# Attention outputs turned by 32x32 block transposes on VectorE instead of transposes on TensorE, in a one-core decoder layer

## The chip, the core and the metric

The kernel runs on one core of a Trainium2 chip. A core has TensorE (matmuls and its own transposes, PE in the rows, with its weight loads as PEld), VectorE (DVE), ScalarE (ACT), GpSimd (POOL) and SyncE (SP, which issues most transfers). Each engine works through its own queue in order and waits on semaphores that the others raise. The metric is the device time of one execution in microseconds (us); lower is better.

## What is computed

One post-norm decoder layer on 16 sequences of 256 tokens with 256 features and 16 heads of 16 features: causal self attention with normalised and rotated queries and keys, causal cross attention to a second sequence with a key mask, and a feed-forward part of two branches (1024 and 128 wide). Cut to what matters here:

```python
qkv = x @ w_qkv.T                       # split into q, k, v of 16 heads
attn = softmax(q @ k.T * 16 ** -0.5)    # causal, per head
out = einsum('bhqk,bhkd->bhqd', attn, v)
out = out.transpose(0, 2, 1, 3).reshape(B, T, 256)
x1 = layernorm(x + out @ w_proj.T)      # self attention; the cross attention
x2 = layernorm(x1 + cross @ Wo)         # is the same with k, v of the context
x3 = layernorm(x2 + ffn(rmsnorm(x2)))
```

## The kernel before

Everything of one sequence (a "batch" b) stays in SBUF. Each engine's program is one Python function `step(i)`, written out for i = -2 to 19, and the order within it is set by hand. In step i the batches are s = i for self attention, c = i - 1 for cross attention, f = i - 2 for the end of cross attention, l = i - 3 for the feed-forward part, and i + 1 and i + 2 for the next q, k and v.

TensorE's step has four phases of 16 heads each, called here **S1** (scores of self attention for s), **S2** (scores of cross attention for c), **T1** (transposed scores of s, which become probabilities) and **T2** (transposed scores of c). Between the heads `phase()` puts other work: for each position h it first issues what tables like `OUT1_AT`, `QK1_AT` or `HIDDEN_AT` assign to h, in the order in which it was added, and then head h. The scores of all phases go round a ring of three PSUM banks (`wait_ring`): a score tile of S1 or S2 may be written when VectorE has taken the maximum (`mx`, L931) of the tile three before it, one of T1 or T2 when ScalarE has taken its exponential (L763). Every matmul is recorded at L359, whatever calls it; the row's tiles tell them apart: `cmaskb,idb` opens a head of S1 or S2, `stk1q,stk1k` and `stk2q,stk2k` are heads of T1 and T2, `pr,va` the values of a group of four heads, `wo,onT` the output projection.

The path of an attention output, for a = 1 (self) and a = 2 (cross): `values` (L530) leaves four groups of four heads with features on partitions, each head in its own 32 of them (16 features, the sum of its probabilities, 15 zeros); ScalarE copies each group to `oT` (`copy_group`, L717). When all four are there, `out_tokens` (L554) turns them to tokens on partitions with eight TensorE transposes (L585), `normalise_heads` on VectorE (L964) takes the reciprocal of the sums and multiplies (L968, L975), `out_dims` (L589) turns the result back with four transposes (L386), ScalarE copies that to `onT` (`copy_out`, L711), and `out_proj` (L595) multiplies with the output weights. For self attention this runs within T2 of the same step: values of the last group at position 3, tokens at 4, back at 8, projection at 10 (`OUT1_AT`); the second half of the q/k projection `qk1` stands at 9. For cross attention it runs in S1 of the next step, at 3, 5, 10 and 12 (`OUT2_AT`).

ScalarE's T2 loop takes, per head, the squares of the q/k projection ahead of heads 5 and 10 (`SQ_AT`, L862) and then the exponential. VectorE's order at the end of a step is: remainder of the cross keys (`take_rest`, L907), `normalise_heads(1, s)`, the split of that remainder, the third layer norm, the two sums of squares (L1037), the residual and statistics of the first layer norm, one Newton step of the inverse root, the first layer norm's output (L1012, which needs a root from GpSimd, L1239), two more Newton steps; then step i + 1 begins with the maxima of S1, with the scaling of q and k at heads 1 and 2, `normalise_heads(2, f)` at head 5 and the split of the cross queries at head 6 (`NORM2_AT`, `SPLITQ_AT`). GpSimd masks each head's probabilities (L1249). SP loads the split q and k of the next batch into `stk1` once T1 is over, and those of cross attention into `stk2`.

Of the kernel before, what the change touches and what calls it, by code (L numbers as in the profile page):

```python
# [56 lines left out]
NG = H // HG  # L57
FCH = 9
# [5 lines left out]
def build(nc, io):  # L64
# [4 lines left out]
    with ctx:  # L69
# [78 lines left out]
        TOK_BANK = (None, (6, 7), (5, 7))  # L148
        DIM_BANK = (None, 5, 5)
# [22 lines left out]
        s_pv = two("out_ready"); s_oT = two("outT_copied"); s_ott = two("outtok_ready")  # L172
        s_rd = two("dve_rden"); s_on = two("on_ready"); s_ont = two("onT_ready"); s_onT = two("onT_copied")
# [183 lines left out]
        def _(pe):  # L357
# [32 lines left out]
            def qk1(b, t):  # L390
# [25 lines left out]
            def k2(b):  # L416
# [3 lines left out]
                if live(b + 1):  # L420
                    pe.wait_ge(s_rest[1], 2 * (b + 1) + 1)
                elif live(b - 2):
                    pe.wait_ge(s_onT[2], b - 1)
# [52 lines left out]
            def transpose_qk1(b):  # L476
                pe.wait_ge(s_rope, TT * (b + 1))

                if live(b - 3):
                    pe.wait_ge(s_onT[2], b - 2)  # L480
# [73 lines left out]
            def out_tokens(a, b):  # L554

                pe.wait_ge(s_oT[a], NG * (b + 1))
                for t in range(TT):
                    if a == 1 and t == 0:
                        if live(b + 1):
                            pe.wait_ge(s_rest[1], 2 * (b + 2))  # L560
                        else:
                            pe.wait_ge(s_rest[2], 2 * b)
                    elif a == 1:
                        if live(b - 2):
                            pe.wait_ge(s_xnT, b - 1)
                        elif live(b - 1):
                            pe.wait_ge(s_mT[2], b)
                        elif live(b + 1):
                            pe.wait_ge(s_qn, TT * (b + 2))
                    elif t == 0:  # L570
                        if live(b + 3):
                            pe.wait_ge(s_va[1], b + 4)
                        elif live(b + 1):
# [820 lines left out]
```

## Time and profile before

| | us |
|---|---|
| three runs, median (lowest to highest) | 995.03 (992.27 to 995.65) |
| the profiled execution | 991.54 |
| its span, first to last instruction | 989.80 |
| TensorE busy in the span | 903.1 |
| VectorE busy | 731.6 |
| ScalarE, GpSimd busy | 495.7, 498.5 |
| mean granted TensorE clock | 0.966 of full |

Busy time of TensorE counts a matmul from its issue to its last result, and neighbours overlap, so a busy TensorE need not be one that never waits; starts of consecutive rows tell more. From about 210 to 815 us the profile repeats itself every 55 us, once per step; one such step, from 375 to 430 us, is read in detail below. Times in rows are us from the span's start unless marked ns.

### The profile page before, as it was taken

The numbers are of one execution on the slowest core, as the hardware profiler recorded it, in microseconds if no ns is written. First come the engines' busy times: TensorE is split into PE (matmuls) and PEld (weight loads), VectorE is DVE, ScalarE is ACT, GpSimd is POOL, SyncE is SP. The second block draws the span as 40 slices with busy tenths as digits, with TensorE's granted clock in tenths as the row PEclk, the third lists the DMA queues.
The fourth block names the chain that finished last, engine by engine and source line by source line (L and its number), as shares of the span: only waits on it lengthen the run. The fifth ranks groups of instructions, "written<-read, shape, count | busy, mean of one in ns | idle before, by whom it ended". The sixth has DMA issues, their size and how long they took to land.

```text
span 989.8 us, 21917 instructions
## 1 busy us (share of the span) xinstructions
PE 903.1 (91%) x7904; PEld 707.7 (71%) x7904; DVE 731.6 (74%) x1842; ACT 495.7 (50%) x1063; POOL 498.5 (50%) x905
## 2 busy tenths in 40 slices
PE   3367888999999999999999999999999999898886
PEld 2335565787878787787878787877878787776676
DVE  7777678677878878877878788887777788574612
ACT  1132443646465555646475655546464655446342
POOL 6454464545555564645464655646455555243221
PEclk8669899999999999999999999999999999999998
DMA  3884091936657290927566381918465572804000
GB/s 108 122 167 67 20 134 22 125 38 98 77 65 109 39 135 10 130 39 108 67 87 88 49 125 25 129 25 120 54 95 81 66 97 37 127 3 76 13 1 22
DMA packets 79644, 74.24 MB, mean 75 GB/s; under 512 B 8592, under 2 KB 78896, under 8 KB 79536
## 3 DMA queue, kind: packets, MB, share of 16 engines
q1 hardware_dynamic: 75008, 68.11, 48.9%
q10 hardware_dynamic: 4528, 4.73, 1.9%
q8 instruction: 63, 1.03, 0.5%
q14 instruction: 45, 0.37, 0.2%
HBM read 17.49 MB, written 4.20 MB: 22 GB/s over the span
## 4 chain that ended last, share of the span: by engine, by line
PE 55%; DVE 20%; issue 8%; DMA 7%; SPq 4%; POOL 3%; ACT 2%; ACTq 0%; POOLq 0%; DVEq 0%
PE bank L359 52%; DVE mx L931 9%; DMA stk1k<-nat1k 4%; SPq L282 4%; POOL pr L1249 2%; PE bank L386 2%; DVE qn L1064 2%; ACT pr L763 1%; PE bank L585 1%; DVE x L1012 1%; DMA stk2k<-nat1k 1%; POOL rstd L1239 1%; DVE nat2q L914 1%; DVE nat2q L916 1%; DVE rest L907 1%
## 5 line engine op out<-in xcount | busy, mean ns | idle before, releaser
L763 ACT ACTIVATE pr<-bank 128x384 f32<-128x384 f32 x512 | 241.1, 502 | 194.3 <-PE bank L359 194.0
L931 DVE TENSOR_REDUCE mx<-bank 128x3 f32<-128x384 f32 x512 | 264.3, 550 | 81.8 <-PE bank L359 80.1
L1249 POOL TENSOR_SCALAR_AFFINE_SELECT pr<-pr 128x256 f32<-128x256 f32 x512 | 226.7, 454 | 184.5 <-ACT pr L763 181.6
L359 PE MATMUL bank<-cmaskb,idb 128*128 128x256 bf16 x512 | 144.4, 282 | 32.9 <-DMA stk2k<-nat1k 13.9
L359 PE MATMUL bank<-w,g 128*128 128x256 f32 x576 | 170.8, 389 | 1.1 <-ACT g L775 1.1
L775 ACT ACTIVATE g<-bank,b 128x256 f32<-128x256 f32 x144 | 68.2, 474 | 91.6 <-PE bank L359 91.3
L1273 POOL TENSOR_TENSOR xTlow<-xT,xThigh 128x512 fp32r<-128x512 f32 x16 | 20.7, 1297 | 149.4 <-ACT xThigh L699 149.4
L359 PEld LDWEIGHTS bank<-w,g 128*128 128x128 f32 x576 | 89.6, 190 | 5.2 <-ACT g L775 1.5
L359 PEld LDWEIGHTS bank<-cmaskb,idb 128*128 128x128 bf16 x512 | 50.2, 98 | 59.5 <-DVE mx L931 28.7
L359 PE MATMUL bank<-stk2k,stk2q 97*128 97x128 bf16 (+1 forms) x512 | 85.1, 253 | 0.0
L359 PE MATMUL bank<-stk1k,stk1q 97*128 97x128 bf16 (+1 forms) x512 | 82.3, 248 | 0.0
L359 PE MATMUL bank<-stk1q,stk1k 100*128 100x256 bf16 (+1 forms) x512 | 79.0, 251 | 2.5 <-ACT pr L763 1.0
L359 PE MATMUL bank<-stk2q,stk2k 100*128 100x256 bf16 (+1 forms) x512 | 73.8, 255 | 4.0 <-DMA stk2q<-mT 3.5
L359 PEld LDWEIGHTS bank<-stk1q,stk1k 100*128 100x128 bf16 x512 | 41.9, 99 | 36.0 <-ACT pr L763 9.3
L359 PE MATMUL bank<-xnh,w1h 128*128 128x256 f32 x288 | 65.2, 308 | 2.3 <-DVE y L984 2.1
L359 PEld LDWEIGHTS bank<-stk2k,stk2q 97*128 97x128 bf16 x512 | 52.0, 102 | 19.1
L259 POOL TENSOR_TENSOR qc<-qn,ropeC 128x256 f32<-128x256 f32 x60 | 44.3, 738 | 41.8 <-DVE qn L1064 41.8
L359 PE MATMUL bank<-wo,onT 128*128 128x256 f32 x256 | 63.2, 391 | 1.9 <-ACT onT L699 1.9
L263 POOL TENSOR_TENSOR sq<-qn,ropeS 128x128 f32<-128x128 f32 x120 | 61.4, 532 | 0.0
L359 PEld LDWEIGHTS bank<-stk2q,stk2k 100*128 100x128 bf16 x512 | 37.6, 100 | 29.1 <-issue 14.1
L359 PE MATMUL bank<-xnl,w1h 128*128 128x256 f32 x288 | 58.2, 284 | 0.0
L1239 POOL TENSOR_TENSOR rstd<-ve,minus_half 128x2 f32<-128x2 f32 x48 | 33.3, 693 | 49.5 <-DVE ve L997 49.5
(159 smaller groups left out, 1870.8 us busy)
## 6 DMA issues: line engine op xcount, KB each, us to landing
stk1q<-nat1q SPq DMA_DIRECT2D x90, 128.0 KB, 4.3
stk1k<-nat1k SPq DMA_DIRECT2D x90, 128.0 KB, 6.6
stk2k<-nat2k SPq DMA_DIRECT2D x90, 128.0 KB, 4.5
stk2q<-nat2q SPq DMA_DIRECT2D x90, 128.0 KB, 6.0
xT<-in_xT SPq DMA_DIRECT2D x16, 256.0 KB, 7.6
ctxT<-in_ctxT SPq DMA_DIRECT2D x16, 256.0 KB, 7.7
x<-in_x SPq DMA_DIRECT2D x16, 256.0 KB, 6.2
out_x<-x SPq DMA_DIRECT2D x16, 256.0 KB, 5.8
```

The source lines that it names most:

```text
L259: ops.tensor_tensor(qc[:, t, s * D:(s + 1) * D].rearrange("p (h d) -> p h d", d=HD), qn[:, t, s * D:(s + 1) * D].rearrange("p (h d) -> p h ...
L263: last = ops.tensor_tensor(rv[:, s, :, half, :], qv[:, s, :, 1 - half, :], ropeS[:, t, s:s + 1, half * h2:(half + 1) * h2] .to_broadcast([ ...
L282: sp.dma_start(dst, src).then_inc(s, 16)
L359: return nc.tensor.matmul(out, lhsT, rhs, start=start, stop=stop, skip_group_check=check)
L386: last = nc.tensor.transpose(bank[k][:, c * T + t * P:c * T + (t + 1) * P], src[:, t, c * P:(c + 1) * P], idf[:, :])
L763: nc.scalar.activation(pr[:, h % (2 * HG), :], ring_bank("T", a, b, h)[:, 0:3 * P], ACT.Exp, scale=HD ** -0.5)\
L775: nc.scalar.activation(g[:, j, :], bank[HIDDEN_BANK[j % 2]][:, 0:T], ACT.Gelu, bias=b1[:, j:j + 1])\
L931: V.tensor_reduce(mx3[:, h, :], scored[:, 0:3 * P].rearrange("p (k t) -> p k t", k=3), AX.X, ALU.max, negate=True).then_inc(s_mx[a], 1)
L1064: V.tensor_tensor(qn[:, t, :].rearrange("p (h d) -> p h d", d=HD), bank[QK1_BANK[t]][:, :].rearrange("p (h d) -> p h d", d=HD), rr[:, t, : ...
L1239: G.tensor_tensor(out, base, minus_half[:, 0:w], ALU.pow)\
L1249: G.affine_select(out=slot, in_=slot, compare_op=ALU.is_ge, fill=0.0, base=0, pattern=[[0, 2], [1, P]], channel_multiplier=-1).then_inc(s_ ...
L1273: G.tensor_tensor(xTp[1][:, :, :], xT[:, :, :], xTp[0][:, :, :].bitcast(f32), ALU.subtract)\
```

## The change

The eight transposes to tokens, the four back and ScalarE's copy are gone from each attention output. In their place VectorE works in two "pairs" of head groups (`normalise_pair`): a block transpose of `oT`'s two groups (128 x 512, each 32x32 block turned in place), the reciprocal and the product, now out of SBUF, and a block transpose of 256 columns into `onT`. Since blocks stay where they are, the features of a pair come out in another order, and the output weights' rows are put in that order on the host (`by_blocks`). "Divided in between" is the division by the sums, between the two transposes. Pair 0 and pair 1 of self attention stand around `take_rest`; pair 0 of cross attention stands at the end of VectorE's step, pair 1 at head 5 of the next S1. The self projection moves from position 10 to 9 of T2, behind `qk1`; the cross projection from 12 to 11 of S1. Waits that had protected the PSUM banks of the transposes are replaced by others. The scratch for dynamic transfers is made smaller, which gives room for the new tile `tok`.

```diff
 NG = H // HG
+NB = T // VW
+PG = NG // C
...
-        oT = sb("oT", [P, NG, T])
-        rden = [None] + [sb(f"rden{a}", [P, TT, H]) for a in (1, 2)]
-        on = sb("on", [P, TT, D])
+        oT = sb("oT", [P, NG, T]); tok = sb("tok", [P, NG, T])
+        rden = [None] + [sb(f"rden{a}", [P, NG, NB]) for a in (1, 2)]
+        on = sb("on", [P, C, T])
...
-                if t == 1 and live(b - 2):
-                    pe.wait_ge(s_on[1], TT * (b - 1))
+                if t == 1 and live(b - 4):
+                    pe.wait_ge(s_xnT, b - 3)
+                elif t == 1 and live(b - 3):
+                    pe.wait_ge(s_mT[2], b - 2)
...
-                    pe.wait_ge(s_onT[1], b - 1)
+                    pe.wait_ge(s_rest[2], 2 * (b - 2) + 1)
...
-            def out_tokens(a, b):
...
-                    for gr in range(NG):
-                        last = nc.tensor.transpose(bank[TOK_BANK[a][t]][:, gr * P:(gr + 1) * P],
-                                                   oT[:, gr, t * P:(t + 1) * P], idf[:, :])
-                    last.then_inc(s_ott[a], 1)
...
-            def out_dims(a, b):
-                pe.wait_ge(s_on[a], TT * (b + 1))
-                if a == 1:
-                    pe.wait_ge(s_rest[2], 2 * b + 1)
-                four_transposes(DIM_BANK[a], on).then_inc(s_ont[a], 1)
-
             def out_proj(a, b):
                 if first(b):
                     pe.wait_ge(s_wcross, 16 * N_CROSS)
-                pe.wait_ge(s_onT[a], b + 1)
+                if a == 1:
+                    if live(b + 1):
+                        pe.wait_ge(s_rest[1], 2 * (b + 2))
+                    else:
+                        pe.wait_ge(s_rest[2], 2 * b)
+                else:
+                    if live(b + 3):
+                        pe.wait_ge(s_qn, TT * (b + 4))
+                    else:
+                        wait(pe, s_xnT, b)
+                pe.wait_ge(s_onT[a], C * (b + 1))
...
-                    add(OUT2_AT[1], out_tokens, 2, f)
-                    add(OUT2_AT[2], out_dims, 2, f)
-                    add(OUT2_AT[3], out_proj, 2, f)
+                    add(OUT2_AT[1], out_proj, 2, f)
...
-                    add(OUT1_AT[1], out_tokens, 1, s)
-                    add(OUT1_AT[2], out_dims, 1, s)
                 if live(i + 2) and not first(i + 1):
                     add(QK1_AT[1], qk1, i + 2, 1)
                 if live(s):
-                    add(OUT1_AT[3], out_proj, 1, s)
+                    add(OUT1_AT[1], out_proj, 1, s)
...
-            def copy_out(a, b):
-                act.wait_ge(s_ont[a], b + 1)
-
-                wait(act, s_o[a], b)
-                copy_dims(onT[a], DIM_BANK[a]).then_inc(s_onT[a], 1)
...
-                wait(act, s_ott[a], TT * b)
-                if a == 1:
-                    wait(act, s_ott[2], TT * (b - 1))
-                else:
-                    wait(act, s_ott[1], TT * (b + 2) if live(b + 1) else TT * B)
+                pair = gr // PG
+                if a == 1 and live(b - 2):
+                    act.wait_ge(s_tok[2], C * (b - 2) + pair + 1)
+                elif a == 1 and live(b - 1):
+                    act.wait_ge(s_tok[1], C * (b - 1) + pair + 1)
+                elif a == 2 and live(b + 1):
+                    act.wait_ge(s_tok[1], C * (b + 1) + pair + 1)
+                elif a == 2:
+                    act.wait_ge(s_tok[2], C * (b - 1) + pair + 1)
...
-            def normalise_heads(a, b):
-                for t in range(TT):
-                    dve.wait_ge(s_ott[a], TT * b + t + 1)
-                    o = bank[TOK_BANK[a][t]][:, :].rearrange("p (h w) -> p h w", w=VW)
-                    V.reciprocal(rden[a][:, t, :], o[:, :, HD]).then_inc(s_rd[a], 1)
-                    dve.wait_ge(s_rd[a], TT * b + t + 1)
-                    wait(dve, s_ont[a], b)
-                    if a == 1:
-                        wait(dve, s_ont[2], b - 1)
-                    else:
-                        wait(dve, s_ont[1], b + 2 if live(b + 1) else B)
-                    V.tensor_tensor(on[:, t, :].rearrange("p (h d) -> p h d", d=HD), o[:, :, 0:HD],
-                                    rden[a][:, t, :].rearrange("p (h o) -> p h o", o=1).to_broadcast([P, H, HD]),
-                                    ALU.mult).then_inc(s_on[a], 1)
+            def normalise_pair(a, b, pair):
+
+                n = C * b + pair + 1
+                groups = slice(PG * pair, PG * (pair + 1))
+                dve.wait_ge(s_oT[a], NG * b + PG * (pair + 1))
+                if a == 1 and live(b - 2):
+                    dve.wait_ge(s_on[2], n - 2 * C)
+                    dve.wait_ge(s_onT[2], n - 2 * C)
+                elif a == 1 and live(b - 1):
+                    dve.wait_ge(s_on[1], n - C)
+                    dve.wait_ge(s_onT[1], n - C)
+                elif a == 2 and live(b + 1):
+                    dve.wait_ge(s_on[1], n + C)
+                    dve.wait_ge(s_onT[1], n + C)
+                elif a == 2:
+                    dve.wait_ge(s_on[2], n - C)
+                    dve.wait_ge(s_onT[2], n - C)
+                V.transpose(tok[:, groups, :].rearrange("p g t -> p (g t)"),
+                            oT[:, groups, :].rearrange("p g t -> p (g t)")).then_inc(s_tok[a], 1)
+                dve.wait_ge(s_tok[a], n)
+                o = tok[:, groups, :].rearrange("p g (k w) -> p g k w", w=VW)
+                V.reciprocal(rden[a][:, groups, :], o[:, :, :, HD]).then_inc(s_rd[a], 1)
+                dve.wait_ge(s_rd[a], n)
+                V.tensor_tensor(on[:, pair, :].rearrange("p (k g d) -> p g k d", g=PG, d=HD), o[:, :, :, 0:HD],
+                                rden[a][:, groups, :].rearrange("p g (k o) -> p g k o", o=1)
+                                .to_broadcast([P, PG, NB, HD]), ALU.mult).then_inc(s_on[a], 1)
+                dve.wait_ge(s_on[a], n)
+                wait(dve, s_o[a], b)
+                V.transpose(onT[a][:, pair, :], on[:, pair, :]).then_inc(s_onT[a], 1)
...
-                        normalise_heads(2, f)
+                        normalise_pair(2, f, 1)
...
+                    normalise_pair(1, s, 0)
                     take_rest(2, s, 1, 0)
-                    normalise_heads(1, s)
+                    normalise_pair(1, s, 1)
                     split_rest(2, s, 1, 0)
...
                     newton(i + 2, 2)
+                if live(c):
+                    normalise_pair(2, c, 0)
...
-X1T_AT, OUT2_AT, Q2_AT = 1, (3, 5, 10, 12), 4
+X1T_AT, OUT2_AT, Q2_AT = 1, (3, 11), 4
...
-K2_AT, OUT1_AT, QK1_AT, V1_AT = 1, (3, 4, 8, 10), (3, 9), 13
-
-COPY2_AT, COPY_XN_AT, COPY_V1_AT = 4, 13, 15
-COPY1_AT, SQ_AT = (0, 3, 3, 9), (5, 10)
+K2_AT, OUT1_AT, QK1_AT, V1_AT = 1, (3, 9), (3, 9), 13
+
+COPY_XN_AT, COPY_V1_AT = 13, 15
+COPY1_AT, SQ_AT = (0, 3, 3), (5, 10)
...
+    def by_blocks(w):
+
+        return w.reshape(C, PG, HG, HD, D).transpose(0, 2, 1, 3, 4).reshape(D, D)
...
-    nc = _bacc.Bacc("TRN2", target_bir_lowering=False, num_devices=1)
+    nc = _bacc.Bacc("TRN2", target_bir_lowering=False, num_devices=1, dynamic_dma_scratch_size=1024)
```

## Rows read from the trace of the kernel before

**Rows 1.** Page, part 1: busy us, share of the span, instructions of each engine.
```profile
PE 903.1 (91%) x7904; PEld 707.7 (71%) x7904; DVE 731.6 (74%) x1842; ACT 495.7 (50%) x1063; POOL 498.5 (50%) x905
```

**Rows 2.** Steady 55 us piece: span, engines' busy us, TensorE's granted clock, DMA share.
```profile
375.00:430.00 55.00, 54.28 (x494) 43.23 (x494) 44.06 (x113) 30.87 (x67) 30.51 (x56) 1.00 0.58 79
```

**Rows 3.** Waits: engine, line, releaser, total us, times, longest.
```profile
PEld bank L359 <- DMA stk1k<-nat1k: 5.5, 7, 2.3
```

**Rows 4.** Chain of waits, one step's T2: start, us, what.
```profile
398.52 0.88 PE bank L585 x8
...
400.95 0.44 PE bank L386 x4
```

**Rows 5.** Timeline of TensorE, same T2: start, us, engine, line, operation, count [idle].
```profile
399.83 0.86 PE L359 MATMUL bank<-pr,va 128*32 128x256 f32 x16
...
402.86 0.34 PE L359 MATMUL bank<-stk2q,stk2k 100*128 100x256 bf16 x2
403.04 1.95 PE L359 MATMUL bank<-wo,onT 128*128 128x256 f32 x8
```

**Rows 6.** Timeline of TensorE: heads 9, 10 of self scores; head 9 next step.
```profile
419.21 0.28 PE L359 MATMUL bank<-cmaskb,idb 128*128 128x256 bf16 x1 [0.23 <-DVE mx L931]
...
419.94 0.27 PE L359 MATMUL bank<-cmaskb,idb 128*128 128x256 bf16 x1
...
474.34 0.28 PE L359 MATMUL bank<-cmaskb,idb 128*128 128x256 bf16 x1 [0.23 <-DVE mx L931]
```

**Rows 7.** Timeline of VectorE, end of T2 and start of S1.
```profile
397.21 0.69 DVE L907 TENSOR_TENSOR rest<-bank,nat2k 128x512 f32<-128x512 f32 x1 [0.86 <-ACT nat2k L699]
399.00 0.26 DVE L968 RECIPROCAL rden<-bank 128x16 f32<-128x16 f32 x1 [1.10 <-PE bank L585]
399.29 0.42 DVE L975 TENSOR_TENSOR on<-bank,rden 128x256 f32<-128x256 f32 x1
399.63 0.25 DVE L968 RECIPROCAL rden<-bank 128x16 f32<-128x16 f32 x1
...
404.25 0.69 DVE L1037 TENSOR_REDUCE ss<-sq 128x32 f32<-128x512 f32 x1 [1.27 <-ACT sq L862]
...
407.27 0.17 DVE L997 TENSOR_SCALAR ve<-mv 128x2 f32<-128x2 f32 x1
...
408.56 1.04 DVE L1012 TENSOR_SCALAR x<-y,mv,rstd 128x256 f32<-128x256 f32 x2 [0.36 <-POOL rstd L1239]
...
418.61 2.40 DVE L931 TENSOR_REDUCE mx<-bank 128x3 f32<-128x384 f32 x5
```

**Rows 8.** Timelines of ScalarE and GpSimd, same T2.
```profile
399.12 0.41 POOL L1249 TENSOR_SCALAR_AFFINE_SELECT pr<-pr 128x256 f32<-128x256 f32 x1 [1.30 <-ACT pr L763]
...
403.63 0.59 ACT L862 ACTIVATE sq<-bank 128x512 f32<-128x512 f32 x1
...
407.84 0.69 POOL L1239 TENSOR_TENSOR rstd<-ve,minus_half 128x2 f32<-128x2 f32 x1
```

**Rows 9.** Groups by shape: busy us, mean ns, idle before; prices of like operations.
```profile
L1037 DVE TENSOR_REDUCE ss<-sq 128x32 f32<-128x512 f32 x32 | 21.6, 680 | 19.2 <-ACT sq L862 19.2
...
L914 DVE CAST nat1k<-rest 128x512 bf16<-128x512 f32 x16 | 6.8, 427 | 0.5
...
L259 DVE TENSOR_TENSOR qc<-qn,ropeC 128x256 f32<-128x256 f32 x4 | 1.7, 420 | 0.0
...
L916 DVE TENSOR_TENSOR nat2q<-rest,nat2q 128x512 bf16<-128x512 f32 x16 | 13.3, 829 | 0.6
```

**Rows 10.** Pieces and TensorE timeline around two earlier waits.
```profile
145.00:151.00 6.00, 5.26 (x20) 4.37 (x21) 3.16 (x7) 0.69 (x2) 3.44 (x6) 0.50 1.14 124
...
850.00:856.00 6.00, 6.00 (x59) 5.08 (x58) 3.79 (x10) 2.86 (x4) 0.04 (x1) 1.00 0.70 118
...
145.74 0.39 PE L359 MATMUL bank<-cmaskb,idb 128*128 128x256 bf16 x1 [2.22 <-DVE mx L931]
...
849.62 0.28 PE L359 MATMUL bank<-cmaskb,idb 128*128 128x256 bf16 x1 [2.12 <-DMA stk1k<-nat1k]
```

More of the change, by code:

```diff
@@ L147, in build @@
         MAX_BANK = (None, 3, 7)
-        TOK_BANK = (None, (6, 7), (5, 7))
-        DIM_BANK = (None, 5, 5)
         PROJ_BANK = (None, 6, 7)
@@ L171, in build @@
         s_st = two("scoresT_ready"); s_exp = two("exp_ready"); s_prob = two("probs_ready")
-        s_pv = two("out_ready"); s_oT = two("outT_copied"); s_ott = two("outtok_ready")
-        s_rd = two("dve_rden"); s_on = two("on_ready"); s_ont = two("onT_ready"); s_onT = two("onT_copied")
+        s_pv = two("out_ready"); s_oT = two("outT_copied"); s_tok = two("outtok_ready")
+        s_rd = two("dve_rden"); s_on = two("on_ready"); s_onT = two("onT_ready")
         s_o = [None, sem("proj1_ready"), sem("proj2_ready"), sem("ffn_ready")]
@@ L421, in k2 @@
                     pe.wait_ge(s_rest[1], 2 * (b + 1) + 1)
-                elif live(b - 2):
-                    pe.wait_ge(s_onT[2], b - 1)
+                elif live(b - 1):
+                    pe.wait_ge(s_rest[2], 2 * (b - 1) + 1)
                 for m in range(C):
@@ L552, in values @@
                 last.then_inc(s_pv[a], 1)
-            def out_tokens(a, b):
-                pe.wait_ge(s_oT[a], NG * (b + 1))
-                for t in range(TT):
-                    if a == 1 and t == 0:
-                        if live(b + 1):
-                            pe.wait_ge(s_rest[1], 2 * (b + 2))
-                        else:
[L562 to L573, printed above, removed]
-                            pe.wait_ge(s_onT[1], b + 2)
-                        else:
-                            wait(pe, s_onT[2], b)
-                    else:
-                        if live(b + 3):
-                            pe.wait_ge(s_qn, TT * (b + 4))
-                        elif live(b + 1):
-                            pe.wait_ge(s_on[1], TT * (b + 2))
-                        else:
-                            wait(pe, s_xnT, b)
-                    for gr in range(NG):
-                        last = nc.tensor.transpose(bank[TOK_BANK[a][t]][:, gr * P:(gr + 1) * P],
-                                                   oT[:, gr, t * P:(t + 1) * P], idf[:, :])
-                    last.then_inc(s_ott[a], 1)
-            def out_dims(a, b):
-                pe.wait_ge(s_on[a], TT * (b + 1))
-                if a == 1:
-                    pe.wait_ge(s_rest[2], 2 * b + 1)
-                four_transposes(DIM_BANK[a], on).then_inc(s_ont[a], 1)
             def out_proj(a, b):
@@ L799, in step @@
                 for j in range(FCH):
-                    if j == COPY2_AT and live(f):
-                        copy_out(2, f)
                     if live(l):
@@ L1374 @@
         "mask": a["mask_BxS2_if1"],
-        "wqk1": a["L0_attn_w_qkv"][:2 * D].T, "wv1": a["L0_attn_w_qkv"][2 * D:].T, "wo1": a["L0_attn_w_proj"].T,
-        "wq2": by_pairs(a["L0_xattn_Wq"]), "wk2": by_pairs(a["L0_xattn_Wk"]), "wv2": a["L0_xattn_Wv"], "wo2": a["L0_xattn_Wo"],
+        "wqk1": a["L0_attn_w_qkv"][:2 * D].T, "wv1": a["L0_attn_w_qkv"][2 * D:].T, "wo1": by_blocks(a["L0_attn_w_proj"].T),
+        "wq2": by_pairs(a["L0_xattn_Wq"]), "wk2": by_pairs(a["L0_xattn_Wk"]), "wv2": a["L0_xattn_Wv"], "wo2": by_blocks(a["L0_xattn_Wo"]),
         "w1h": a["L0_ffn_w1_h"].T, "w1l": a["L0_ffn_w1_l"].T, "w2h": a["L0_ffn_w2_h"].T, "w2l": a["L0_ffn_w2_l"].T,
```

8 lines of the change are left out of this document (removed).

## The prediction

> **What bounds the kernel now.** I read the busy shares first [rows 1], then the steady stretch cut into pieces of 55 us [rows 2], the waits [rows 3], and then one step instruction by instruction. Over the span TensorE is busy 91% [rows 1]; in a steady piece it is busy 54.28 of 55.00 us and VectorE 44.06 [rows 2]. TensorE's wait in front of head 9 of the self scores comes back after one step: 419.21 and 474.34 [rows 6], 55.1 apart. So the first reading is "TensorE is the bound, whatever leaves it is won". The second reading is more careful. That same row says what TensorE waits for at 419.21: VectorE's head maxima [rows 6]. From 408.56 (the first layer norm's output) to 418.61 VectorE's queue has no idle time in front of any instruction [rows 7], and the score tiles sit in a ring of three banks, so head 9 needs the maximum of head 6. The step therefore has two parts: from about 419 round to the end of the cross stage T2 TensorE sets the pace, and from the layer norm at 408.56 to head 9 VectorE sets it, with TensorE idle only some tenths because both are nearly equal there. The idle times of VectorE (0.86, 1.10, 1.27, 0.36) all lie before or at 408.56 [rows 7].
>
> **What leaves TensorE.** Each attention output loses eight transposes (0.88 us) and four (0.44) [rows 4], 1.32; a step has two, 2.64 of 55. ScalarE loses two 128x512 copies a step; it idles a great deal, so I count nothing. If nothing else were late, 16 steps would give 42 us.
>
> **What VectorE gets.** Instead of two reciprocals and two products per attention (starts at 399.00, 399.29, 399.63: 0.63 for one of each, 1.26 for two) [rows 7] there are two "pairs", each a transpose of 512 columns, a reciprocal, a product and a transpose of 256. The trace has no transpose on VectorE, so it is bounded by neighbours: a one-source 512-element reduce out of SBUF takes 680 ns, the fastest 512-element one-source op 427 [rows 9]; for 256 elements the VectorE product takes 420 [rows 9]. I take 0.68 and 0.42, since an op that moves each column once is nearest to the reduce; the low end is 0.43 and 0.27, the high end twice the taken values (each 4-byte element in two passes; no row excludes it). Nothing below that: these are added instructions on a queue that runs one at a time. A dependent op starts 0.03 after the one before it ends, an independent one 0.08 before (399.00 with 0.26, then 399.29 with 0.42, then 399.63) [rows 7]. So a pair is 0.71+0.28+0.45+0.34 = 1.78. The product now reads both operands from SBUF; a 512-element subtract that does so takes 829 ns, 149 more than the one-source reduce [rows 9]. I add half of it, 0.07 (bounds 0 and 0.15): **1.85 a pair**, bounds 1.38 and 3.0.
>
> The Trainium skill ("VectorE: DVE Perf Modes", The three transpose paths) gives 311 ns for a 128x128 bf16 transpose on VectorE against 390 on TensorE; an estimate from it, one more column a cycle at that page's 0.96 GHz, is 0.71 and 0.44, which would put 0.05 more on a pair and about 1.3 us on the total. No row here shows it. The skill also says ("SBUF — State Buffer", Who interferes with whom) that a VectorE instruction with two SBUF inputs contends with a GpSimd instruction that reads SBUF, which speaks against moving the product's operand out of PSUM; the 829 against 680 agrees in direction [rows 9].
>
> **Where the four pairs of a step lie.** Two for self attention, around the cross-key remainder: from the end of the third layer norm's statistics on VectorE has idle times of 0.86, 1.10 and 1.27 = 3.23 before 404.25 [rows 7]. The added work there is 2 x 1.85 - 1.26 = 2.44: hidden, VectorE would be ready for the second sum of squares at about 403.3. One cross pair stands right after the Newton steps, ahead of the maxima, where nothing hides it; the other stands at head 5, in place of the old products (1.26).
>
> **A move that costs.** The self output projection goes from in front of head 10 to in front of head 9 of T2, behind the second q/k projection. ScalarE's queue is in order: the exponential of head 9, then the second squares (403.63) [rows 8], which feed the second sum of squares. Old: the values of cross group 0 start at 399.83 and head 9 at 402.86, 3.03 apart, 0.44 of it the dropped transposes [rows 4, 5]. New: the values can start once head 3 is masked on GpSimd (399.12 + 0.41) [rows 8], about 399.6, only 0.23 earlier although 0.88 is gone; 2.59 later, 402.2, stands the projection (1.95, its last 0.17 overlapped [rows 5]), and head 9 comes at about 404.0 where it was at 402.86: **1.13 later**. The second squares are late by that, the second sum starts at 405.38, and with it all that follows in order: residual, statistics, the variance. GpSimd's root (407.84, 0.69) [rows 8] stood behind a mask, 0.40 after the variance (407.27 + 0.17) [rows 7]; now the variance is the later one: 407.44 + 1.13 = 408.57, and 0.69 and two hand-overs behind it the layer norm's output starts at about 409.36 instead of 408.56: +0.80. VectorE's own queue gives the same, 1.13 less the 0.36 that it sat idle there [rows 7].
>
> **The sum for one step**, taken at the end of VectorE's stretch: +0.80 (squares), +1.85 (cross pair 0), +1.85 - 1.26 = +0.59 (cross pair 1): the maximum of head 6 moves from 418.61 by 3.24. Head 10 stood at 419.94 behind the dropped transposes [rows 6]; now it waits for the maximum of head 7, which ended at 419.64 (418.61, a fifth of 2.40, and 0.55) [rows 7], so it stands at 422.9: **+2.95**. Behind it TensorE's work to the next T2 is as long as before (the cross projection only moves within it). The saved 1.32 of T2 buys nothing: the next self scores also need stack transfers which SP issues only after T1's end and which TensorE already waits for in seven places [rows 3]. Full steps are 13 (steps 1 to 13, which have squares to come and a cross pair): 13 x 2.95 = 38.4. The first self output and the last three outputs have no such stretch behind them and keep their gain: 4 x 1.32 = 5.3 off. Net +33. The profiled execution took 991.54 us (span 989.8); +33 gives 1024.7. The median of the runs shown, 995.03, is 0.35% higher: **1028**.
>
> Edits with no cost: the output weights' rows are reordered on the host, the new token tile and the smaller scratch hold no work. New waits: the q/k projection on the low half of the normed x (done 394.5, needed 400.7), the value projection on the cross-key remainder (398.7, needed 405), ScalarE's group copies on the token transposes (about 397 and 399.5, needed 401 and in the next step; the exponentials are queued behind them), the projection on both self pairs (400.6, needed 402.2). With the long transposes that last cover is gone and costs some tenths.
>
> **Rivals.** *TensorE stays the bound* (not slower). Its place is the start of the self scores. The change of a step is s + 2p - 1.26 - 0.30, s the shift of the layer norm, p the pair, 0.30 what head 10 had to spare. With s = +0.80 it is zero at p = 0.38, less than reciprocal and product alone (0.73). If the squares were not held behind the projection, s would be about -1.2 (1.0 from the second sum, the rest from the 0.36), and it turns at p = 1.38, the low bound. With p = 1.0 a step wins 0.76: 13 x 0.76 + 5.3 = 15, 980 us. For it speaks TensorE's 54.28 of 55; against it the rows with no idle on VectorE. 9%.
> *The squares are not late but pairs cost what I take*: +0.94 a step, 12.2 - 5.3, 1002 us. Against it: both queues are in order. 8%.
> *The clock falls.* In an early self-score stage TensorE already stood 2.22 us behind VectorE's maxima, and the granted clock was 0.50 in the 6 us after, the lower level, 1.2 GHz [rows 10]; in the steady piece it is 1.00 [rows 2]. The forecast makes two waits of about 2 us in every step (before heads 3 and 9). If the clock falls there each time, the cross query projection (1.7 us at full clock) takes 1.7 more ahead of VectorE's head 4, up to 3 with the 6 us: 13 x 1.7 to 3 = 22 to 39 more, 1050 to 1067. Against it: another wait of 2.12 us, before 849.62, left the clock at 1.00 [rows 10]. 19%.
> *Transposes take two passes*: p = 3.0, 2.3 more a step, 1058. 8%.
>
> **How the numbers follow.** The forecast keeps 56%, with 1012 to 1042 from the pair's bounds near 1.5 and 2.3. The range 1002 to 1058 leaves out the first rival (9), part of the clock's (about 8) and little else. A measurement here can tell 0.3% from no change. Faster: nearly all of the first rival, 8%; same: its edge and that of the second, 5%; slower 87%.
>
> **What would show it.** After: steps of about 58 us; the wait before head 9 some 2 us instead of 0.23, released by the maxima; VectorE without idle time from the layer norm to there; the second sum of squares still waiting for ScalarE, by 1 to 2 us; TensorE's busy share lower by about 7 points. I am wrong if a 512-column transpose is far from 0.68, if the second squares come before 404, or if the granted clock is below 1.00 in the steady pieces.

## The result and the profile after

The changed kernel takes 1029.44 us (median of four runs, 1029.26 to 1031.19) against 995.18 of the kernel before, a ratio of 1.0355 (95% interval 1.0332 to 1.0377): it is slower by 3.5%. The forecast was 1028. The profiled execution took 1029.26 us, its span is 1027.5; before it was 991.54 and 989.80, so 37.7 us have to be found in the traces.

First the busy shares of the changed kernel (page, part 1: busy us, share of the span, instructions):

```profile
PE 875.9 (85%) x7520; PEld 669.6 (65%) x7520; DVE 800.3 (78%) x1970; ACT 475.3 (46%) x1031; POOL 501.7 (49%) x905
```

One steady piece of it (span, busy us of PE, PEld, DVE, ACT and POOL with their instructions, granted clock, DMA share, GB/s):

```profile
390.00:448.00 58.00, 52.49 (x472) 40.81 (x470) 48.49 (x121) 29.65 (x65) 30.85 (x56) 1.00 0.48 75
```

TensorE's 91% of [rows 1] has become 85%: it has 27 us less work and 38 us more span. VectorE gained 68.7 us of work. The clock of the steady piece is 1.00 as in [rows 2], so the clock is not where these steps lose. Steady steps take 57.93 us each; they took 55.00.

What TensorE waits for (engine and line, releaser: total us, times, longest):

```profile
PEld bank L359 <- DVE mx L889: 77.8, 94, 2.4
PE bank L359 <- DVE mx L889: 55.5, 48, 2.2
```

The same two rows of the kernel before, where the maxima are line 931:

```profile
PEld bank L359 <- DVE mx L931: 30.0, 73, 2.6
PE bank L359 <- DVE mx L931: 13.1, 32, 2.4
```

The maxima are where TensorE now stands. Next TensorE in one step, from the first head of T2 to head 10 of the self scores (start, us, engine, line, operation, tiles, shape, count, idle time before and its releaser):

```profile
409.10 0.33 PE L359 MATMUL bank<-stk2q,stk2k 100*128 100x256 bf16 x2
...
417.47 1.89 PE L359 MATMUL bank<-wo,onT 128*128 128x256 f32 x8
...
424.38 0.28 PE L359 MATMUL bank<-cmaskb,idb 128*128 128x256 bf16 x1 [0.58 <-DMA stk1k<-nat1k]
...
429.55 0.28 PE L359 MATMUL bank<-cmaskb,idb 128*128 128x256 bf16 x1 [1.93 <-DVE mx L889]
...
437.72 0.28 PE L359 MATMUL bank<-cmaskb,idb 128*128 128x256 bf16 x1 [1.52 <-DVE mx L889]
...
438.18 0.28 PE L359 MATMUL bank<-cmaskb,idb 128*128 128x256 bf16 x1
```

This step's T2 starts at 409.10, the first row; the one read before the change started 15.32 earlier:

```profile
393.78 0.33 PE L359 MATMUL bank<-stk2q,stk2k 100*128 100x256 bf16 x2
```

Taking off 15.32 makes the two steps comparable: head 9 moved from 419.21 to 422.40 and head 10 from 419.94 to 422.86 [rows 6]. The two waits, 1.93 before head 3 and 1.52 before head 9, are what 0.23 has become. VectorE in the same stretch:

```profile
420.57 0.69 DVE L1010 TENSOR_REDUCE ss<-sq 128x32 f32<-128x512 f32 x1 [1.98 <-ACT sq L820]
...
424.68 0.88 DVE L985 TENSOR_SCALAR x<-y,mv,rstd 128x256 f32<-128x256 f32 x2 [0.17 <-POOL rstd L1215]
...
427.12 0.70 DVE L939 STREAM_TRANSPOSE tok<-oT 128x512 f32<-128x512 f32 x1
427.86 0.25 DVE L943 RECIPROCAL rden<-tok 128x16 f32<-128x16 f32 x1
428.14 0.42 DVE L945 TENSOR_TENSOR on<-tok,rden 128x256 f32<-128x256 f32 x1
428.60 0.45 DVE L950 STREAM_TRANSPOSE onT<-on 128x256 f32<-128x256 f32 x1
428.97 0.52 DVE L889 TENSOR_REDUCE mx<-bank 128x3 f32<-128x384 f32 x1
...
432.51 0.70 DVE L939 STREAM_TRANSPOSE tok<-oT 128x512 f32<-128x512 f32 x1
...
433.54 0.80 DVE L945 TENSOR_TENSOR on<-tok,rden 128x256 f32<-128x256 f32 x1
...
434.74 0.52 DVE L889 TENSOR_REDUCE mx<-bank 128x3 f32<-128x384 f32 x1
...
437.11 2.40 DVE L889 TENSOR_REDUCE mx<-bank 128x3 f32<-128x384 f32 x5
```

From 424.68 on no row has an idle time in front of it, as in [rows 7] from 408.56 on, and both cross pairs stand in this stretch. In front of the second sum of squares VectorE still has 1.98 us idle: there the two self pairs are hidden.

The chain of work that ended last shows the whole path through one step, here from the values ahead of T2's head 9 to GpSimd's root, which the first layer norm needs (start, us, what):

```profile
414.89 4.64 PE bank L359 x36
419.56 0.04 ACT pr L725
...
419.95 0.60 ACT sq L820
...
423.95 0.70 POOL rstd L1215
```

The chain goes through TensorE's matmuls up to head 9, the self projection among them, the exponential of that head, the second squares behind it, the second sum, and with it the residual, the statistics and GpSimd's root.

### The profile page after: what moved, and what is told of

Its sections match the earlier page's. It is cut to its first block, busy times and chain, and to the rows that moved or that the text cites. A ratio compares the mean times of both kernels' runs of the same rounds, so it can differ in the third digit from the quotient of the medians.

```text
span 1027.5 us, 21257 instructions
## 1 busy us (share of the span) xinstructions
PE 875.9 (85%) x7520; PEld 669.6 (65%) x7520; DVE 800.3 (78%) x1970; ACT 475.3 (46%) x1031; POOL 501.7 (49%) x905
## 4 chain that ended last, share of the span: by engine, by line
PE 51%; DVE 29%; issue 9%; POOL 4%; DMA 3%; ACT 3%; SPq 1%; ACTq 0%; POOLq 0%; DVEq 0%
PE bank L359 50%; DVE mx L889 9%; POOL pr L1225 2%; DVE tok L939 2%; ACT pr L725 2%; DVE on L945 2%; DVE x L985 2%; DVE qn L1037 1%; DVE y L957 1%; DVE st L964 1%; POOL rstd L1215 1%; DMA stk2k<-nat1k 1%; DVE nat2q L874 1%; DVE rest L865 1%; DVE ss L1010 1%
## 5 line engine op out<-in xcount | busy, mean ns | idle before, releaser
L259 POOL TENSOR_TENSOR qc<-qn,ropeC 128x256 f32<-128x256 f32 x60 | 49.5, 824 | 72.4 <-DVE qn L1037 72.4
L359 PE MATMUL bank<-stk2q,stk2k 100*128 100x256 bf16 (+1 forms) x512 | 69.2, 255 | 8.4 <-ACT pr L725 4.9
L1215 POOL TENSOR_TENSOR rstd<-ve,minus_half 128x2 f32<-128x2 f32 x48 | 33.3, 695 | 64.8 <-DVE ve L970 64.8
L359 PE MATMUL bank<-pr,va 128*32 128x256 f32 (+1 forms) x1024 | 56.8, 341 | 4.5 <-POOL pr L1225 2.1
```

The source lines that it names most:

```text
L259: ops.tensor_tensor(qc[:, t, s * D:(s + 1) * D].rearrange("p (h d) -> p h d", d=HD), qn[:, t, s * D:(s + 1) * D].rearrange("p (h d) -> p h ...
L359: return nc.tensor.matmul(out, lhsT, rhs, start=start, stop=stop, skip_group_check=check)
L1215: G.tensor_tensor(out, base, minus_half[:, 0:w], ALU.pow)\
```

## The experiments

The theory is the prediction's: the step is longer by what VectorE gets between the layer norm and the maximum of head 6, and by the delay of the squares behind the projection; the same work elsewhere costs nothing. The rivals change from test to test. All kernels but the one before are edits of the changed kernel. Times are medians, ratios are against the kernel before, run on the same chip beside them (993.77 us beside the first four kernels, 992.33 beside the last four).

| kernel | us | ratio (95%) | usual step at clock 1.00, head 9 to head 9 |
|---|---|---|---|
| before | 995.18 | 1 | 55.00 |
| changed | 1029.44 | 1.0355 (1.0332 to 1.0377) | 57.93 |
| e1, projection at 10 | 1007.92 | 1.0134 (1.0103 to 1.0166) | 56.50 |
| e2, both cross pairs at head 5 | 1069.87 | 1.0742 (1.0691 to 1.0794) | none at 1.00 |
| e3, cross pairs at 5 and 11 | 1009.77 | 1.0153 (1.0122 to 1.0185) | 56.37 |
| e4, e1 and e3 together | 996.10 | 1.0015 (0.9996 to 1.0035) | 54.90, in 5 of 11 |
| e5, self transposes twice | 1039.69 | 1.0467 (1.0439 to 1.0495) | 58.15 |
| e6, cross transposes twice | 1092.39 | 1.0997 (1.0964 to 1.1030) | none at 1.00 |
| e7, cross pairs at 3 and 5 | 1042.52 | 1.0497 (1.0464 to 1.0531) | 57.80, in 4 of 11 |
| e8, cross pairs at 9 and 13, projection at 10 | 987.48 | 0.9939 (0.9918 to 0.9960) | 54.2 to 55.6 |

### The self projection back behind head 9 (e1)

```diff
-K2_AT, OUT1_AT, QK1_AT, V1_AT = 1, (3, 9), (3, 9), 13
+K2_AT, OUT1_AT, QK1_AT, V1_AT = 1, (3, 10), (3, 9), 13
```

> The changed kernel with one number changed: the self output projection goes back in front of head 10 of T2. Theory (the step's +2.93 us is the sum of late squares and of cross pairs in VectorE's uncovered stretch): head 9 and behind it ScalarE's second squares come 1.7 us earlier; the layer norm's output then waits for GpSimd's mask of head 12 and comes 1.5 earlier; step 57.93 to about 56.4, total 1029.4 - 13 x 1.5 = 1010 (1006 to 1014). Rival (VectorE's added work costs the time wherever it lies, the projection's place does not matter): 1029.

Measured 1007.92, as expected. VectorE's rows of one step whose T2 starts at 398.61:

```profile
408.38 0.69 DVE L1010 TENSOR_REDUCE ss<-sq 128x32 f32<-128x512 f32 x1 [0.28 <-ACT sq L820]
...
412.70 1.04 DVE L985 TENSOR_SCALAR x<-y,mv,rstd 128x256 f32<-128x256 f32 x2 [0.36 <-POOL rstd L1215]
```

The idle time in front of the second sum is 0.28 where it was 1.98, and the layer norm's output stands 14.09 after T2's start (412.70 - 398.61) where it stood at 15.58 in the changed kernel: 1.49 earlier, and the step is 1.43 shorter. So one number in a table is worth 21 of the 34 us. That is more than the 0.80 that the forecast charged to the squares, because with the projection in its old place the layer norm also comes 0.69 earlier than in the kernel before (14.78 there), where the transposes that were dropped still stood in front of the squares.

### Cross pair 0 away from the end of the step (e2, e3)

Two kernels take cross pair 0 from the step's end. In the first it joins pair 1 at head 5:

```diff
                 def normalise_cross():
                     if live(f):
+                        normalise_pair(2, f, 0)
                         normalise_pair(2, f, 1)
...
-                if live(c):
-                    normalise_pair(2, c, 0)
```

> The changed kernel with cross pair 0 moved from the end of the step to head 5 of the next S1, beside pair 1: the same work between the layer norm and the maximum of head 6, in another place. Theory: TensorE's wait of 1.93 us before head 3 goes and comes back before heads 8 and 9; step 57.9, total 1029 (1025 to 1033). Rival (what costs is that the maxima start 1.85 later): 57.93 - 1.85, total 1005.

It took 1069.87: neither. TensorE's rows in one of its steps:

```profile
569.30 0.28 PE L359 MATMUL bank<-cmaskb,idb 128*128 128x256 bf16 x1 [1.40 <-DVE mx L889]
...
572.08 0.40 PE L359 MATMUL bank<-cmaskb,idb 128*128 128x256 bf16 x1 [2.33 <-DVE mx L889]
...
573.12 3.62 PE L359 MATMUL bank<-wo,onT 128*128 128x256 f32 x8
```

and the seven us from there beside the six after (columns as above):

```profile
571.00:578.00 7.00, 5.92 (x21) 4.96 (x22) 2.93 (x6) 0.00 (x0) 2.37 (x3) 0.52 0.65 131
578.00:584.00 6.00, 6.00 (x58) 5.70 (x57) 3.88 (x12) 3.44 (x6) 0.00 (x0) 1.00 0.00 0
```

The sum of the two waits, 3.73, is near the 3.45 of the changed kernel (1.93 and 1.52, with 6.7 us between the end of one and the start of the other). But here they stand almost side by side, 0.45 us apart; the granted clock behind them is 0.52, nearly all of it at the lower of its two levels, 1.2 GHz, and the cross projection takes 3.62 us where it takes 1.89 at full clock. All steady steps have one such fall or two, of 3.4 or 6.8 us each. The step from 452.39 to 512.07 (the products of head 9) has a single one, 451.8 to 455.2, and takes 59.68, 1.75 above 57.93: about half of 3.4 us, which is what half the clock takes when TensorE has work all the while. With that taken off, the theory's arithmetic on VectorE holds in this step; it left out that the place of a wait can cost more than its length.

In the second kernel pair 1 moves on to head 11, pair 0 takes its place at head 5, and the cross projection goes to 15:

```diff
-QN_AT, NORM2_AT, SPLITQ_AT, RESID2_AT, MAXT_AT, STAT2_AT = (1, 2), 5, 6, 1, 3, 6
+QN_AT, NORM2_AT, SPLITQ_AT, RESID2_AT, MAXT_AT, STAT2_AT = (1, 2), (5, 11), 6, 1, 3, 6
...
-X1T_AT, OUT2_AT, Q2_AT = 1, (3, 11), 4
+X1T_AT, OUT2_AT, Q2_AT = 1, (3, 15), 4
...
-                if live(c):
-                    normalise_pair(2, c, 0)
```

> The changed kernel with cross pair 0 at head 5 and pair 1 at head 11 of S1, and the cross projection at position 15: one pair leaves the stretch between the layer norm and the maximum of head 6 and stands where VectorE waits for TensorE. Theory: head 9 comes 2.2 earlier (pair 1 took 2.23 there), step about 55.7, total 1029.4 - 13 x 2.2 = 1001 (996 to 1007). Rival (added work costs wherever it lies): 1029.

Measured 1009.77. The direction is the theory's, the size is short: a step is 1.56 shorter. VectorE in one of its steps:

```profile
641.88 0.88 DVE L985 TENSOR_SCALAR x<-y,mv,rstd 128x256 f32<-128x256 f32 x2 [0.17 <-POOL rstd L1215]
...
652.49 2.40 DVE L889 TENSOR_REDUCE mx<-bank 128x3 f32<-128x384 f32 x5
...
655.84 1.18 DVE L945 TENSOR_TENSOR on<-tok,rden 128x256 f32<-128x256 f32 x1
```

and TensorE in the same step:

```profile
653.10 0.28 PE L359 MATMUL bank<-cmaskb,idb 128*128 128x256 bf16 x1 [1.53 <-DVE mx L889]
...
658.00 0.28 PE L359 MATMUL bank<-cmaskb,idb 128*128 128x256 bf16 x1 [0.29 <-DVE mx L889]
```

From the layer norm to head 6's run of maxima VectorE needs 10.61 us (652.49 - 641.88) where the changed kernel needed 12.43 (437.11 - 424.68): 1.82 less, one pair. But pair 1 at head 11 lets a later head wait 0.29 (658.00), and 1.82 - 0.29 = 1.53 is about what the step won (1.56). The expected 2.2 was the price of pair 1, but what left the stretch is one pair of 1.82: the pair that stays at head 5 still costs the 0.80 of its product. The product of pair 1 at head 11 took 1.18; GpSimd's 1.28 us sum `x2b`, which starts at 655.45, runs beside it.

### e1 and e3 together (e4)

> Both edits: pairs at heads 5 and 11, cross projection at 15, self projection at 10. Theory: 1.5 + 2.2 = 3.7 less VectorE time ahead of head 9, bounded by TensorE's own work (its waits add up to 4.8 us a step in the changed kernel, 0.6 of them for a transfer); step 54.2 to 54.7, total 975 to 990, below the kernel before. Rival (added work costs wherever it lies): 1029.

Measured 996.10, the time of the kernel before (the interval reaches from 0.9996 to 1.0035). The two edits' gains, 1.43 and 1.56, add up to 2.99, and the usual step went from 57.93 to 54.90, 3.03 less: in that step they are independent, as two terms of one sum should be. The totals do not add: alone the edits won 21.5 and 19.7 us, together 33.3. Only five of the eleven steps from head 9 of batch 3 on take 54.9; two take 57.15 and 57.17 with a fall of the clock, two 56.00 without one (why stays open) and two 54.46, together 5.9 us more than eleven times 54.90. My figure of 975 to 990 took the sum of expected gains, not of measured ones, and no such steps. In a step from 633 to 688 us TensorE still waits for maxima, 1.38 us before head 9 (at 643.99) and 0.26 at 648.87.

### The same work in two places (e5, e6)

Each 512-column transpose is issued a second time, for self attention in one kernel (a == 1), for cross attention in the other (a == 2). Both get the same instructions in the same number.

```diff
+                if a == 1:
+                    V.transpose(tok[:, groups, :].rearrange("p g t -> p (g t)"),
+                                oT[:, groups, :].rearrange("p g t -> p (g t)")).then_inc(s_again[a], 1)
+                    dve.wait_ge(s_again[a], n)
                 V.transpose(tok[:, groups, :].rearrange("p g t -> p (g t)"),
                             oT[:, groups, :].rearrange("p g t -> p (g t)")).then_inc(s_tok[a], 1)
```

> Each 512-column transpose of a self pair is issued twice (the second writes the same values again); the cross pairs are as in the changed kernel. That adds 2 x (0.70 + 0.03) = 1.46 us a step to VectorE, in the stretch in which the changed kernel's VectorE sits idle 1.98 us in front of the second sum of squares. Theory of the prediction (work of VectorE costs nothing there, because ScalarE's squares end that stretch): 1029, within 1026 to 1033; the second sum starts at the same place in the step and the idle time in front of it falls to about 0.5. The self pair 1 then ends about when the self projection is due, which may cost a tenth. Rival (VectorE has become the bound of the whole step, so any instruction on it is paid): 16 x 1.46 = 23 more, 1052.

> The same edit on the cross pairs: each of their 512-column transposes is issued twice, the self pairs are as in the changed kernel. Same instructions, same number: 1.46 us a step more on VectorE, but between the layer norm's output and the maximum of head 6. Theory of the prediction: every step is longer by 1.46, 13 x 1.46 = 19, 1048 (1044 to 1054), if the granted clock stays at 1.00 in the steady steps. If the longer waits of TensorE (about 2.7 before head 3 and 2.2 before head 9) let the clock fall in the steps, as two waits close together did with both pairs at head 5, 1.7 to 3 a step come on top: 1070 to 1090. Rival (the pairs cost through something else than their time on VectorE): as the other kernel of this pair, 1029.

The self copy took 1039.69, 10.3 more than the changed kernel, the cross copy 1092.39, 63 more. The self copy's steps at full clock are 58.15, 0.22 longer for 1.46 us of work, and its rows show where the 0.22 may come from, VectorE's first and then TensorE's (a step whose T2 starts at 647.44):

```profile
655.36 0.45 DVE L954 STREAM_TRANSPOSE onT<-on 128x256 f32<-128x256 f32 x1
...
659.13 0.69 DVE L1014 TENSOR_REDUCE ss<-sq 128x32 f32<-128x512 f32 x1 [0.86 <-ACT sq L820]
```

```profile
655.95 1.96 PE L359 MATMUL bank<-wo,onT 128*128 128x256 f32 x8
```

VectorE still sits idle 0.86 in front of the second sum, so its own queue has room. But the self projection starts behind the end of pair 1 (655.36 + 0.45), 8.51 after T2's start, where it started 8.37 after it, and takes 0.07 longer: the cover that the prediction called gone with long transposes. The spans are 10.7 apart. Thirteen times 0.22 is 2.9 of it; 2.7 are there by head 9 of batch 2 and 2.6 come behind head 9 of batch 15, in the first and last steps; why they cost more there stays open. The remaining 2.5 lie in two steps of 59.24 and 59.64 us in which the clock fell for 3.4 us. Neither number that was written down fits the total; the steady step is nearly the theory's.

The cross copy's longer waits are 2.68 before head 3 and 2.34 before head 9, 0.75 and 0.82 more than in the changed kernel, one transpose each:

```profile
574.02 0.28 PE L359 MATMUL bank<-cmaskb,idb 128*128 128x256 bf16 x1 [2.68 <-DVE mx L889]
...
583.26 0.38 PE L359 MATMUL bank<-cmaskb,idb 128*128 128x256 bf16 x1 [2.34 <-DVE mx L889]
```

So 1.46 is paid in full, 59.39 would be the step. Every steady step has at least one fall of the clock, and they take from 61.0 to 64.8; one with a single fall (521.9 to 525.3) takes 61.05, 1.66 above 59.39. The same two instructions a step cost 0.22 in the one place (a usual step) and between 3 and 7 in the other, the clock's falls included: a VectorE microsecond has no fixed price here.

### Are two waits dearer when they stand together? (e7)

Pair 0 at head 3, pair 1 at head 5, the rest as in the changed kernel.

> Cross pair 0 goes from the end of VectorE's step to ahead of the maximum of head 3 and pair 1 stays at head 5; nothing else. In the kernel with both pairs at head 5 two waits of 1.4 and 2.3 us stood 0.4 us of work apart, the granted clock fell to 0.50 behind them in each step, and it took 1070. Here the maxima of heads 3 and 4 and, on TensorE, some 3 to 4 us of work lie between the two pairs. Theory (the work of VectorE is the same as in the changed kernel, and the 41 us came from the clock, which fell because the waits stood together): steps of about 58 us with clock 1.00 in most, 1029 (1024 to 1037). Rival (the 41 us come from having no pair at the step's end, whatever the distance of the two): 1060 to 1075.

It took 1042.52, between the two. Of the eleven steps from head 9 of batch 3 on, four take 57.79 to 57.81, the theory's, with the clock at 1.00; six take 59.31 to 60.54 and have a fall. TensorE's rows of one step of each kind, and then three pieces (columns as above):

```profile
557.58 0.28 PE L359 MATMUL bank<-cmaskb,idb 128*128 128x256 bf16 x1 [2.06 <-DVE mx L889]
...
616.90 0.28 PE L359 MATMUL bank<-cmaskb,idb 128*128 128x256 bf16 x1 [2.06 <-DVE mx L889]
```

```profile
323.40:381.50 58.10, 53.95 (x471) 41.57 (x472) 48.38 (x121) 29.57 (x64) 30.99 (x58) 0.97 0.49 75
555.00:562.00 7.00, 4.87 (x21) 3.73 (x22) 4.32 (x9) 0.14 (x1) 4.47 (x6) 0.76 0.65 131
615.00:662.00 47.00, 43.78 (x394) 33.68 (x394) 37.92 (x96) 24.69 (x56) 22.74 (x42) 1.00 0.43 66
```

The first piece is the one step of the eleven that is left, at 0.97: it has a fall of 3.4 us too, from 370.1 on, and takes 58.05, only 0.24 more than the four at 1.00. Behind that fall TensorE's waits for maxima add up to 1.07 us less than in the next step (0.39 and 0.45 are gone, 2.06 is 1.83): what the clock took came in part out of time in which TensorE would have waited. Behind the wait of 2.06 at 557.58 the clock fell, behind an equal one 59 us later it did not. Pulling the two waits apart thus took most of the 41 us away (13 are left), and the length of the wait in front does not tell by itself whether the clock falls. What else decides stays open.

### A version that is faster than both (e8)

The pairs go behind the maximum of head 6, to heads 9 and 13, the cross projection to the end of the self scores, the self projection to 10.

```diff
-QN_AT, NORM2_AT, SPLITQ_AT, RESID2_AT, MAXT_AT, STAT2_AT = (1, 2), 5, 6, 1, 3, 6
+QN_AT, NORM2_AT, SPLITQ_AT, RESID2_AT, MAXT_AT, STAT2_AT = (1, 2), (9, 13), 6, 1, 3, 6
...
-X1T_AT, OUT2_AT, Q2_AT = 1, (3, 11), 4
+X1T_AT, OUT2_AT, Q2_AT = 1, (3, 16), 4
...
-K2_AT, OUT1_AT, QK1_AT, V1_AT = 1, (3, 9), (3, 9), 13
+K2_AT, OUT1_AT, QK1_AT, V1_AT = 1, (3, 10), (3, 9), 13
...
-                if live(c):
-                    normalise_pair(2, c, 0)
```

> Against the kernel with the cross pairs at heads 5 and 11 and the self projection at head 10 (996): the pairs go to heads 9 and 13, behind the maximum of head 6 that releases head 9, and the cross projection to the end of the self scores. In that kernel TensorE still waited 1.4 us for the maxima before head 9, and behind head 9 VectorE had some 2 us of idle time (1.16 before head 15's maximum, 0.15 in front of each of six maxima of the cross scores). Theory (only what stands between the layer norm and head 6's maximum is paid): the wait before head 9 is gone, steps of 53.4 to 54.3, 975 to 988, faster than the kernel before. Rival (VectorE is short through the whole stage of self scores, so that the wait comes back before heads 12 to 15): steps of 54.9 as there, 996.

Measured 987.48 against 992.33, a ratio of 0.9939 (0.9918 to 0.9960): faster than the kernel before by 0.6%, than the changed kernel by 4%. TensorE's largest remaining waits in one step, and then the shares of the chain of work that ended last:

```profile
637.87 0.28 PE L359 MATMUL bank<-cmaskb,idb 128*128 128x256 bf16 x1 [0.64 <-DVE mx L889]
...
641.19 1.97 PE L359 MATMUL bank<-wo,onT 128*128 128x256 f32 x8 [0.41 <-DVE onT L950]
...
680.98 0.28 PE L359 MATMUL bank<-cmaskb,idb 128*128 128x256 bf16 x1 [0.87 <-DMA stk1k<-nat1k]
```

```profile
by line: PE bank L359 44.3%; DMA stk1k<-nat1k 8.4%; SPq L282 8.1%; DVE mx L889 7.4%; issue 7.1%; POOL pr L1225 2.0%; PE bank L386 2.0%; DVE tok L939 2.0%; DVE on L945 1.7%; DVE onT L950 1.3%; ACT pr L725 1.3%; DMA stk2k<-nat1k 1.2%; DVE nat
```

The wait before head 9 is gone, as the theory said, and 0.64 before head 12 and 0.41 before the projection stand for it. But the steady steps shrank by about 0.2 only (head 9 of batch 2 to head 9 of batch 15: 712.5 us, before 713.2; a gain of 3.3 us was there by batch 2). What bounds it now can be read in the last row of TensorE: the next self scores wait 0.87 for the transfers of `stk1`, the longest such wait from 210 to 830 us. SP issues them one after another when T1 ends, in that step from 665.51 to 673.66, and the last takes 7.22 more. From T1's last head to the first self score of the next step are 14.8 to 15.8 us here and 15.5 to 16.3 in the kernel before (ten steps each, means 15.4 and 15.7), though T2 lost 1.32 us of transposes. In the chain those transfers and their issue are 16.5% (8.4 and 8.1), before 7.8%. No run moved the transfers, so this bound is read from the trace and not tested; from 210 to 830 us TensorE also still waits for maxima, 9.9 us against 5.1 for `stk1`.

## Why the prediction was right, step by step

**The pair: right where nothing runs beside it.** Forecast 1.85 us; pair 0 took 1.85 (427.12 to 428.97), pair 1 2.23 (432.51 to 434.74). The group rows of the changed kernel (busy us, mean ns, idle before):

```profile
L939 DVE STREAM_TRANSPOSE tok<-oT 128x512 f32<-128x512 f32 x64 | 45.0, 703 | 10.2 <-ACT oT L663 10.2
L945 DVE TENSOR_TENSOR on<-tok,rden 128x256 f32<-128x256 f32 x64 | 32.4, 507 | 2.2
L950 DVE STREAM_TRANSPOSE onT<-on 128x256 f32<-128x256 f32 x64 | 28.5, 445 | 2.2
L943 DVE RECIPROCAL rden<-tok 128x16 f32<-128x16 f32 x64 | 16.2, 254 | 2.2
```

Taken were 680 and 420 ns for the transposes, 420 and half of 149 for the product. The estimate from the Trainium skill ("VectorE: DVE Perf Modes", The three transpose paths), 0.71 and 0.44, agrees with 703 and 445, closer than the rows from which I priced them. That pair 0 agrees to the hundredth is luck: the transposes were priced too low by about as much as the 0.07 that I added to its product and that is not there. The two passes of a rival are excluded. The product's extra was taken as a constant and is none: its shortest and median are 424 and 426 ns, its longest 849. At 428.14, with GpSimd idle, it takes 0.42; at 433.54 it takes 0.80 beside GpSimd's rotation of q and k, whose sums `qr` run there from 433.33 for 1.62 us. Of the 64 products 13 took 0.78 to 0.85, eleven beside `qr` and two beside `x2b`; the 17 with GpSimd idle took 0.42 or 0.43, and the 19 beside its masks, which read one tile of SBUF, at most 0.45. The rule of the Trainium skill that I weighed ("SBUF — State Buffer", Who interferes with whom) agrees in direction for GpSimd's sums of two tiles, with up to a doubling here and 1.18 us in one test; beside the masks, which read SBUF too, the trace shows next to nothing of it. The link is read from the times; no run changed GpSimd's work alone.

**The squares: right.** The second sum was to come 1.13 late and came 1.00 late (420.57 - 15.32 = 405.25, before 404.25 [rows 7]); the layer norm's output was to come at 409.36 and came at 409.36 (424.68 - 15.32). That the end agrees to the hundredth is partly luck: the sum came 0.13 earlier than forecast, and the stretch from there to the variance took 0.11 longer, so that the variance came 1.11 late. (VectorE's readiness for that sum comes out of the idle times as 403.46 and not 403.3; nothing hangs on it.) The test with the projection at 10 shows that the projection is the cause.

**The sum for one step: right, with two misses that cancel.** Head 6's run of maxima was to move by 3.24 and moved by 3.18 (437.11 - 15.32 against 418.61); head 10 by 2.95 and moved by 2.92 (438.18 - 15.32 against 419.94). The step took 2.93 more. Pair 1's product cost 0.38 more than pair 0's, and that was made up by the split of the cross queries behind it, whose cast takes 0.44 here and took 0.78; neither was in the sum.

**The whole: short by 4.6 us, and the total near by luck.** Head 9 of batch 1 starts 1.02 earlier than in the kernel before, head 9 of batch 14 38.85 later, that of batch 15 40.18 later, and the end of the span 37.7 later. The thirteen steps from batch 1 to 14 thus cost 39.9, where 13 x 2.95 = 38.4 was forecast; one of them (batch 3 to 4) cost 4.44, 1.5 above the forecast, with a fall of the clock at 254:

```profile
252.00:258.00 6.00, 4.07 (x19) 3.14 (x15) 4.47 (x10) 0.45 (x2) 3.26 (x7) 0.72 0.67 82
```

The fourteenth, which has no squares to come, cost 1.3, and I had counted none for it. The first and last outputs, for which I took 4 x 1.32 = 5.3 off, gave 1.0 and 2.5. All three misses go the same way, 1.5, 1.3 and 1.8, so the span grew by 37.7 and not by 33, and the profiled execution took 1029.26 where the sum gives 1024.7. The forecast of 1028 came near the measured 1029.44 because I had raised 1024.7 by 0.35%, the distance of the profiled execution of the kernel before from its median; the changed kernel's profiled execution lies no lower than its median (1029.26 against 1029.44). The band of 1012 to 1042 for pairs of 1.5 to 2.3 us does not follow from the sum either, which gives 1019 to 1040; the measured time lies in both.

**The saved 1.32 of T2: bought nothing, as said.** The first self score of the step waits 0.58 for `stk1` (424.38), and it starts 15.5 us after T1's last head, as in the kernel before.

**The rivals.** TensorE did not stay the bound. With the squares not held back I had said 1002; the test gave 1008, since the layer norm moved by 0.69 and not by 1.2 (GpSimd's root kept its 0.36 in front of it). The clock's rival did not happen in the changed kernel's steady steps but one, with waits of 1.93 and 1.52; it happened in every steady step of two of its neighbours, whose waits were longer or closer, at 1070 and 1092, and in seven of eleven steps of a third, at 1043. The changed kernel stood near that edge: moving one pair by a few heads crosses it.

## What to carry to other kernels

Before work is moved from a busy engine to one with idle time, find out where in the step the idle time lies: the same 1.46 us a step cost 0.22 in a usual step in front of a wait and 3 to 7 behind it. Whoever moves an instruction on one queue should follow what an in-order queue puts behind it; here one position of the projection was worth 21 us. When the moved work has been placed well, look for the next bound; here the trace points at neither engine but at the transfers that start at the end of a stage.

## What the runs showed of the hardware that was not expected

TensorE's granted clock fell in steady steps once waits for VectorE lay close together or grew: two waits of 1.40 and 2.33 us with 0.45 us between them, or 2.68 and 2.34 with 6.9 between them, came with falls in every steady step, 1.93 and 1.52 with 6.7 between them with a fall in one steady step alone. A fall of 3.4 us cost 1.5 to 1.8 us in three steps looked at (59.44, 59.68 and 61.05), where TensorE had work, which takes about twice as long at the lower level (3.62 us for a projection of 1.89), and 0.24 in a step (58.05) in which TensorE's later waits took up part of it. An equal wait of 2.06 us was followed by a fall in some steps and not in others, so the length of the wait alone does not decide.

A product of two SBUF operands on VectorE took between 0.42 and 1.18 us for the same 256 columns, and the long ones ran beside GpSimd's sums of two tiles.
